# DLRM tower with a recursive field interaction: pair sums in two PSUM banks, the wide bank merged into the outer-product banks, and one of four relus moved to VectorE

## The reference, cut to what matters

```python
xk = x                                              # x: [B, 16, 256]
for i in range(3):
    z = einsum('bfe,bge->bfge', x, xk)              # all pairs of fields
    z = relu(einsum('bcl,oc->bol', z, Ws[i]) + bs[i])   # 256 pairs -> 16 outputs, for each e
    z = sum(z, axis=-1)                             # over e: [B, 16]
    outs.append(z)
    xk = broadcast(z over e)                        # [B, 16, 256]
h = concatenate([outs (48 values), dense_ctx (16)])
h = relu(h @ W_top1 + b1)                           # 64 -> 512
h = relu(h @ W_top2 + b2)                           # 512 -> 256
y = h @ W_top3                                      # 256 -> 1
```

## Time and profile before

| | |
|---|---|
| median of 3 runs | 614.34 us (613.95 to 615.65) |
| profiled execution | 614.28 us, span 612.5 us, mean granted clock 0.989 |
| PE busy | 566.3 us (92% of the span) |
| DVE busy | 494.5 us (81%) |
| ACT busy | 437.6 us (71%) |
| POOL busy | 463.1 us (76%) |

### The profile page before, as it was taken

How to read it: one execution, slowest core, us unless ns; L and a number is a source line. 1 busy time by engine, 2 the same in 40 slices (tenths; PEclk the granted TensorE clock), 3 DMA queues, 4 the chain that set the end, 5 groups by cost and what they waited for, 6 DMA issues and landing times.

```text
span 612.5 us, 18145 instructions
## 1 busy us (share of the span) xinstructions
PE 566.3 (92%) x7680; PEld 329.1 (54%) x7680; DVE 494.5 (81%) x220; ACT 437.6 (71%) x1234; POOL 463.1 (76%) x565
## 2 busy tenths in 40 slices
PE   1778889999999999999999999999999999999776
PEld 1334445555555565655556555555556565555444
DVE  5898899888888988888889888888899888887100
ACT  2466677768778776878878777887877786886542
POOL 5989888888878887888878888888878788862000
PEclk9999899999999999999999999999999999999978
DMA  4422222222222222222222122222222222210000
GB/s 98 115 76 73 62 62 71 61 62 63 61 62 63 61 63 63 61 63 61 63 63 65 58 64 62 60 63 61 63 64 63 68 61 59 59 45 1 1 1 2
DMA packets 14788, 35.89 MB, mean 59 GB/s; under 512 B 5921, under 2 KB 6305, under 8 KB 14689
## 3 DMA queue, kind: packets, MB, share of 16 engines
q0 software_dynamic: 12288, 33.57, 19.3%
q1 hardware_dynamic: 2418, 1.16, 0.8%
HBM read 34.70 MB, written 0.01 MB: 57 GB/s over the span
## 4 chain that ended last, share of the span: by engine, by line
PE 68%; DVE 20%; issue 7%; ACT 3%; POOL 2%; DMA 0%; SPq 0%; DVEq 0%; POOLq 0%; ACTq 0%
PE sum_ps L521 29%; DVE prods L222 19%; PE turn_ps L501 9%; PE outer_ps L564 9%; PE wide_ps L585 7%; PE sum_ps L541 5%; PE wide_ps L576 4%; PE outer_ps L559 3%; ACT relu_k L431 2%; POOL emb L262 2%; PE sum_ps L536 1%; PE wide_ps L593 1%; PE sum_ps L547 0%; PE sum_ps L533 0%; DMA id_lim<-id_limits 0%
## 5 line engine op out<-in xcount | busy, mean ns | idle before, releaser
L222 DVE TENSOR_TENSOR prods<-turn_ps,emb_t 128x3360 f32<-128x3360 f32 x128 | 462.2, 3646 | 11.8 <-ACT emb_t L404 8.9
L262 POOL DMA_INDIRECT emb<-tables,rows_sb x256 | 252.1, 985 | 44.9 <-issue 31.1
L521 PE MATMUL sum_ps<-prods,w_sb 128*32 128x272 f32 x4096 | 267.1, 400 | 2.5 <-POOL prods L222 2.3
L521 PEld LDWEIGHTS sum_ps<-prods,w_sb 128*32 128x32 f32 x4096 | 126.0, 110 | 94.0 <-issue 14.5
L421 ACT ACTIVATE relu<-sum_ps,bias_sb 128x120 f32<-128x120 f32 x256 | 91.8, 370 | 100.8 <-PE sum_ps L521 96.6
L272 POOL TENSOR_TENSOR prods<-emb_t 128x256 f32<-128x256 f32 x128 | 94.8, 741 | 53.8 <-ACT emb_t L404 50.3
L431 ACT ACTIVATE relu_k<-outer_ps 128x2048 f32<-128x2048 f32 x64 | 120.9, 1889 | 4.5 <-PE outer_ps L564 4.4
L501 PE MATMUL turn_ps<-ident_sb,emb 128*128 128x128 f32 x512 | 90.7, 295 | 29.7 <-DVE prods L222 10.9
L403 ACT COPY emb_t<-turn_ps 128x512 f32<-128x512 f32 x128 | 76.1, 595 | 44.2 <-PE turn_ps L501 36.2
L501 PEld LDWEIGHTS turn_ps<-ident_sb,emb 128*128 128x128 f32 x512 | 55.1, 143 | 88.8 <-issue 49.0
L411 ACT ACTIVATE prods<-emb_t 128x512 f32<-128x512 f32 x128 | 83.0, 649 | 0.1
(11 more groups left out here) (41 smaller groups left out, 269.2 us busy)
## 6 DMA issues: line engine op xcount, KB each, us to landing
emb<-tables,rows_sb POOLq DMA_INDIRECT x256
w_sb<-w_top SPq DMA_DIRECT2D x1, 512.0 KB
ids_sb<-ids_t SPq DMA_DIRECT2D x1, 128.0 KB, 2.0
h<-dense_t SPq DMA_DIRECT2D x1, 128.0 KB
w_sb<-w_top SPq DMA_DIRECT2D x1, 128.0 KB
ident_sb<-ident SPq DMA_DIRECT2D x1, 64.0 KB
w_sb<-w_cols SPq DMA_DIRECT2D x1, 64.0 KB
wp_sb<-w_proj SPq DMA_DIRECT2D x1, 32.0 KB
```

Source lines behind the costliest of these rows:

```text
L222: eng.tensor_tensor(out, every, shifted, ALU.mult).then_inc(done, 1)
L262: nc.gpsimd.indirect_dma_start(out=emb[:, k % EMB_RING, t * E:(t + 1) * E], out_offset=None, in_=tables, in_offset=bass.IndirectOffsetOnAx ...
L521: last = nc.tensor.matmul(sum_ps[s * 2 * F:(s + 1) * 2 * F, 0:SUM_COLS], w_sb[:, c, odd, :], x[:, c, 2 * s + odd, :, :], start=c == 0 and ...
```

## The change

- `wide_ps` goes. `project` writes bank 0 of `outer_ps`, the folds banks 0 and 1, `hidden1` banks 2 and 3. The waits of `wait_wide` are replaced by waits in `outer_round` and `project`.
- `sum_ps` gets two banks, by the parity of the slot; the side pieces use the bank of their slot. `turn` now waits for the sums of one slot earlier than before.
- In the second of the two layers ACT takes only the relu of the first round. A new DVE instruction, `relu_add` (slot 19, after `products`), takes the relu of the second round from the four PSUM banks and adds the first round's from SBUF (128x2048). Fold 1 then sums 8 matmuls in place of 16.
- project moves from slot 10 to 11, its transpose from 11 to 12, the second z_spread from 15 to 16, the first reduction from 15 to 16.
- `hidden1` takes its input from two copies of h0 in rows 0 to 63 and 64 to 127, and its four matmuls use the two halves of the array's rows in turn. `z_t` makes both copies with two matmuls of 64 columns, and now transposes the dense inputs too, which are loaded into `z_cat` (128 partitions x 16 groups x 16 floats) and no longer straight into h0. `w_top1` is loaded twice.
- ACT does `relu_hidden1` ahead of `take_turned` in its slot.

```diff
-PROJ, Z0_FIN, TURN_P, Z0_DIAG, Z0_SUM = 10, 9, 11, 9, 10
-Z_BUILD = (11, 15)
+PROJ, Z0_FIN, TURN_P, Z0_DIAG, Z0_SUM = 11, 9, 12, 9, 10
+Z_BUILD = (11, 16)
-REDUCE = (15, 20)
+REDUCE = (16, 20)
+RELU_ADD = 19
+PROJ_BANK, FOLD_BANK, H1_BANK = 0, (0, 1), 2
...
-        sum_ps = ps("sum_ps", [P, 512])
+        sum_ps = ps("sum_ps", [P, 2, 512])
-        wide_ps = ps("wide_ps", [P, 512])
...
-            sp.dma_start(h0[3 * F:, :], dense_t).then_inc(top_in, 16)
+            sp.dma_start(z_cat[:, :, 3 * F:], dense_b).then_inc(top_in, 16)
...
+            def relu_add(g):
+                n = ROUND_NO[1, g, 1]
+                dve.wait_ge(outer_done, n + 1)
+                dve.wait_ge(outer_relu, n)
+                at_least(dve, fold_done[1], g)
+                first, second = (relu_k[:, 1, q, :, :, :].rearrange("p j h n -> p (j h n)") for q in range(TURNS))
+                nc.vector.scalar_tensor_tensor(out=second, in0=outer_ps[:].rearrange("p j n -> p (j n)"), scalar=0.0,
+                                               in1=first, op0=ALU.max, op1=ALU.add).then_inc(outer_relu, 1)
...
-                if slot - 1 in ROUND_AT:
+                if slot - 1 in ROUND_AT and (ROUND_AT[slot - 1][0], ROUND_AT[slot - 1][2]) != (1, 1):
                     relu_round(*ROUND_AT[slot - 1])
-                take_turned(slot + 2)
                 if (g := group_at(slot - 1, HIDDEN1)) is not None:
                     relu_hidden1(g)
+                take_turned(slot + 2)
...
-                at_least(pe, relu0_ready, 3 * min(slot, STEPS))
+                at_least(pe, relu0_ready, 3 * min(slot - 1, STEPS - (slot - STEPS) % 2))
...
-                    if q == 0 and j == 1:
-                        pe.wait_ge(proj_ready, g + 1)
-                    if q == 0 and j == 2:
+                    if q == 0 and j == 0:
+                        pe.wait_ge(proj_ready if k == 0 else z_ready[0], g + 1)
+                    if q == 0 and j == 1 and k == 0:
+                        at_least(pe, z_ready[1], g)
+                    if q == 0 and j == 2 and k == 1:
+                        at_least(pe, h1_ready, H1 * g)
+                    if q == 0 and j == 3:
                         pe.wait_ge(z_wide_ready[k], g + 1)
...
-                for q in range(G4):
+                first = k * HALF_G
+                for q in range(first, G4):
...
                 for i in range(H1):
-                    last = nc.tensor.matmul(wide_ps[:, i * P:(i + 1) * P], w1_sb[:, i * P:(i + 1) * P], h0[:, g * P:(g + 1) * P],
-                                            start=True, stop=True)
+                    rows = slice(i % 2 * CAT, (i % 2 + 1) * CAT)
+                    last = nc.tensor.matmul(outer_ps[:, H1_BANK + i % 2, i // 2 * P:(i // 2 + 1) * P], w1_sb[rows, i * P:(i + 1) * P],
+                                            h0[rows, g % 2, :], start=True, stop=True)
```

More of the change, by code:

```diff
@@ L47 @@
 PT_RING = 2
-CAT_RING = 2
 LEAD = 4
@@ L190, in build @@
         N_OTHER = 3
[L192 to L198, removed]
         def wait_side(eng, slot):
-            before = [(kind, n) for at, kind, n in SIDE_ORDER if at <= slot]
-            if before:
-                kind, n = before[-1]
+            earlier = [(kind, n) for at, kind, n in SIDE_ORDER if at <= slot and (slot - at) % 2 == 0]
+            if earlier:
+                kind, n = earlier[-1]
                 done, count = {"z0": (z0_taken, n + 1), "z_t": (h0_ready, n + 1), "h2a": (h2_ready, H2 * n + 1),
@@ L380, in _ @@
                 products(slot)
+                if (g := group_at(slot, RELU_ADD)) is not None:
+                    relu_add(g)
                 if (g := group_at(slot, Z0_FIN)) is not None:
@@ L529, in side @@
                     wait_sums_read(slot)
-                    wait_side(pe, slot - 1)
+                    wait_side(pe, slot - 2)
                 if what == "z0":
                     pe.wait_ge(diag_ready, g + 1)
-                    nc.tensor.matmul(z0_ps, z0_diag[:], own_sb[:], start=True, stop=True).then_inc(z0_done, 1)
+                    nc.tensor.matmul(sum_ps[:, slot % 2, SUM_COLS:SUM_COLS + F], z0_diag[:], own_sb[:],
+                                     start=True, stop=True).then_inc(z0_done, 1)
                 elif what == "z_t":
                     pe.wait_ge(z_ready[1], g + 1)
-                    nc.tensor.matmul(z_t_ps, z_cat[:, g % CAT_RING, :], ident_sb[:], start=True, stop=True).then_inc(z_t_done, 1)
+                    for half in range(2):
+                        last = nc.tensor.matmul(sum_ps[half * CAT:(half + 1) * CAT, slot % 2, SIDE], z_cat[:, g, :], ident_sb[:],
+                                                start=True, stop=True)
+                    last.then_inc(z_t_done, 1)
                 elif what in ("h2a", "h2b"):
@@ L540, in side @@
                     for a in range(H1):
[L541 removed]
+                        last = nc.tensor.matmul(sum_ps[:, slot % 2, SIDE], w2_sb[:, a, i * P:(i + 1) * P], h1[:, a * P:(a + 1) * P],
                                                 start=a == 0, stop=a == H1 - 1)
@@ L575, in project @@
                     for j in range(J):
-                        last = nc.tensor.matmul(wide_ps[j * R:(j + 1) * R, :], wp_sb[:, c, :],
+                        last = nc.tensor.matmul(outer_ps[j * R:(j + 1) * R, PROJ_BANK, :], wp_sb[:, c, :],
                                                 x[:, j // 2, j % 2, c, :, :, 0:F], start=c == 0, stop=c == EC - 1)
@@ L621, in _ @@
                 sum_pairs(slot)
-                if slot >= STEPS and slot in WIDE_AT:
-                    wait_wide(pe, *WIDE_AT[slot])
-                by_32 = slot in WIDE_AT and WIDE_AT[slot][0] in ("proj", "fold0", "fold1")
-                if by_32:
-                    wide(*WIDE_AT[slot])
+                if (g := group_at(slot, PROJ)) is not None:
+                    project(g)
+                for k in range(2):
+                    if (g := group_at(slot, FOLD[k])) is not None:
+                        fold(k, g)
                 if slot in ROUND_AT:
                     outer_round(*ROUND_AT[slot])
-                if slot in WIDE_AT and not by_32:
-                    wide(*WIDE_AT[slot])
+                if (g := group_at(slot, HIDDEN1)) is not None:
+                    hidden1(g)
 def shape_constants():
```

87 lines of the change are left out of this document (38 added, 49 removed).

## The result

The changed kernel takes 595.59 us (median of 4 runs, 592.63 to 597.39); the kernel before took 614.82 beside it (613.95 to 615.65). The ratio is 0.968, 95% interval 0.963 to 0.973: 3.2% faster. The forecast was 589 with a range of 582 to 604, so the side and the range are right and the size is 6.6 us too hopeful. The four runs lie in two pairs, near 593 at a mean granted clock of 0.991 and near 597 at 0.983; the profiled execution is the 597.39 one, and against the control run further down its extra time is in the tail, where PE has pauses and its clock is low.

A forecast was written before the change was run, and what follows sets the result against it. PE was taken to bound the kernel, with DVE near level after the change (33.0 and 32.9 us a group). Savings of 20.7, 4.4 and 0.8 us gave a 586.6 us span, 588.4 with surroundings, rounded to 589; range 582 to 604.

The forecast's parts named there:

- relu_add, 2.20 us: On DVE, the new 2048-column instruction takes 2.20 us at the rate of products; upper bound 4.3 us.
- first rival: relu_add on DVE runs at half rate, 4.3 us: 35.3 us a group, time about 620 us; chance 0.12.
- DVE's waits give way to work: On DVE, 3.7 us a group of waits for project and the first fold are replaced by 2.2 us of work.
- Fold 1, -0.95: On PE, summing 8 matmuls in place of 16 saves half of 1.91 us, 0.95 us a group.
- The second bank of sums: No price of its own; named only as part of the possible extra gain of 0.4 us a group.
- fourth rival: More than forecast: second bank of sums and ACT's lighter load save 0.4 us a group, about 583 us; chance 0.06.
- hidden1, -0.55: On PE, hidden1's matmuls in two halves of the array nearly fully share it, saving 0.55 us a group.
- third rival: hidden1 doesn't share the array on PE: 15 x 0.55 = +8, about 597 us; chance 0.07.
- The round of the second layer: PE's round in slot 16 waits for hidden1's relus and z_wide; close to a tie, priced at 0.1 us a group.
- second rival: PE waits 0.5 to 1 us a group at the second layer's first round: about 600 us; chance 0.15.
- The period, 33.2 forecast: Groups 1 to 13 go from 34.8 to 33.2 us each, -20.7 us in all.
- Group 0, -4.4 forecast: Group 0 keeps DVE's busy 30.25 us plus some 1 us for ACT's copies: -4.4 us from 35.6.
- After the groups, -0.8 forecast: Six slots after 538.3 us gain from the sooner reduction but lose relu_add: -0.8 us; the tail's -0.6 taken as 0.

The follow-up runs named there:

- control run: The changed kernel unaltered, run again on the same chip as the runs beside it: 595.25 us, ratio 0.971 to the kernel before.
- act_relu: The changed kernel with the fourth round's relu back on ACT and fold 1 summing all 16 matmuls: 600.39 us, ratio 0.982 to the kernel before.
- both_fixes: The changed kernel with finish0's single reduction and the tail's outputs in turn_ps together: 583.17 us, ratio 0.963 to the kernel before.
- add_twice: The changed kernel with relu_add done twice, the first result into a spare buffer: 633.90 us, ratio 1.036 to the kernel before.
- relu_add_alone: The kernel before with only relu_add on DVE at slot 19 and fold 1 halved to 8 matmuls: 621.72 us, ratio 1.015.
- reduce_15: The changed kernel with the first reduction and second z_spread back in slot 15: 610.81 us, ratio 0.995 to the kernel before.
- one_sum_bank: The changed kernel with sum_ps back in one bank and its waits as before: 609.16 us, ratio 1.004 to the kernel before.
- copies_first: The changed kernel with ACT doing take_turned ahead of relu_hidden1 again: 593.72 us, ratio 0.979 to the kernel before.
- one_reduce: The changed kernel with finish0's two DVE instructions replaced by one reduction over 17 columns: 591.03 us, ratio 0.963 to the kernel before.
- tail_banks: The changed kernel with hidden1 of the last three groups and the last project writing turn_ps: 589.31 us, ratio 0.961 to the kernel before.
- port_probe: The changed kernel with one more 16-column DVE product, SBUF to SBUF, after each products, 128 in all: 607.93 us in one execution.

## Why the prediction was right, and where its sum was off

*What bounds the kernel.* PE before, PE and DVE level after: as said. `act_relu` shows PE busy 33.85 of 33.85 and `both_fixes` 32.90 of 32.90, and the forecast of PE's own work was 33.0 us (33.11 busy in the period above). DVE's forecast of 32.9 met its busy time of 32.99 partly by luck: 0.4 of that is the hold of `z_rows`, which I didn't know, and the rest is 0.3 less than I had summed.

*relu_add, 2.20 us.* Measured 2.20 from start to start, 2.28 as its own duration. The first rival is settled: with one source in PSUM and one in SBUF it goes at the 1.04 ns a column of `products`. The Trainium skill, "Vector Engine (DVE) Microarchitecture Reference", section 7, halves this form for two non-bf16 SBUF sources. With one in PSUM the runs show no halving. `add_twice` shows what it would have cost: 3.6% slower.

*DVE's waits give way to work.* Right, no wait for project or the first fold is left. But the prediction told the moves as one item. `relu_add_alone` and `reduce_15` show that the reduction's slot is what makes room: without it the kernel takes 1.5% more and 0.5% less than before.

*Fold 1, -0.95.* Right: 2.00 us to the next start before (305.57 to 307.57), 1.10 after and 1.00 in `both_fixes`.

*The merged bank adds nothing.* Right in the groups. It is also what allows the reduction's move: with one `wide_ps`, hidden1 in slot 15 would have to wait for a reduction in slot 16. That is read from the order of the uses, not tried.

*The second bank of sums.* The prediction names it only in the fourth rival, as a possible extra. The forecast silently took "the side pieces stay as they are" for granted; `one_sum_bank` shows that without this bank they don't, for 0.85 us a group. It takes 15.4 us more than `copies_first`, which ran beside it; 595.6 + 15.4 is 611 us, an estimate, and outside my range. The forecast came out right because the change had the bank, not because I had worked that term out: luck. The fourth rival's extra gain didn't come.

*hidden1, -0.55.* Measured -0.45 (1.09 to 0.64), so the third rival fell. The estimate of -0.41 from the Trainium skill's figure ("TensorE: Matmul & The Clock Gate", part 3) was the closer. It cost 0.1 us a group. My reading of the rounds as nearly fully shared was too high: durations of records overlap without sharing too. hidden1's own eight of 289 ns, 2.3 us, stood in 1.18 us in the earlier trace rows, so the rounds' 6.0 us in 1.03 are a sharing of about 3 of 4, an estimate from these two rows.

*The round of the second layer.* I put 0.1 us a group on the tie; from 100 us on the trace has 0.3 us in one group. The second rival fell in the groups. In the tail, where there are no steps to cover them, the same waits stand.

*The period, 33.2 forecast, 33.45 measured: the largest miss, 4.8 of 20.7 us over the thirteen groups.* A part of it is group 1, which takes 34.52 us (82.73 to 117.25) and has PE's wait of 2.2 us for z_wide in it; the twelve others take 33.49. There DVE's row has 32.6 us of its own work, 0.41 of waiting for ACT's copies and 0.4 by which `z_rows` is held by POOL. The copies I knew from the earlier trace rows and let them be covered. The hold I did not know. `one_reduce` takes the held instruction away and gets 33.18, the forecast's figure, though with less work on DVE than the forecast had. The prediction's "hand-overs that I didn't see" had 0.6 us in the whole sum and needed over 4.

*Group 0, -4.4 forecast, -2.5 measured.* I had left DVE its work and 1 us of waiting. It had 30.83 us of work, 0.8 of it in a `z_rows` of 0.97 us that POOL held, and waited 2.3 us for project. PE came late to project, with waits for POOL before it. From 20 to 95 us:

```profile
PE sum_ps L520 <- POOL prods L208: 7.6, 9, 1.0
...
DVE proj_b L355 <- PE outer_ps L587: 2.3, 1, 2.3
PE outer_ps L568 <- POOL z_wide L283: 2.2, 1, 2.2
```

Of the first row 1.8 us are in this group and 5.8 in the 30 us ahead of it; the last row is in group 1. POOL is busy 30.26 us of this group's 33.14. That POOL is what holds group 0 up rests on the profile alone; no run tests it.

*After the groups, -0.8 forecast, +2.3 in the profiled execution.* The tail's rows:

```profile
549.80 0.39 PE L568 MATMUL outer_ps<-bias_wide,ones_sb 32*128 32x512 bf16 x2 [1.28 <-ACT h L457]
...
554.37 2.29 DVE L365 SCALAR_TENSOR_TENSOR relu_k<-outer_ps,relu_k 128x2048 f32<-128x2048 f32 x1 [5.10 <-PE outer_ps L573]
556.71 3.14 PE L587 MATMUL outer_ps<-emb_t,wp_sb 128*32 128x512 f32 x16 [2.10 <-DVE relu_k L365]
559.60 1.59 PE L597 MATMUL outer_ps<-relu_k,fold_sb 128*32 128x256 f32 x16
...
575.62 0.39 PE L568 MATMUL outer_ps<-bias_wide,ones_sb 32*128 32x512 bf16 x2 [0.92 <-ACT h L457]
```

project stood 2.10 us behind relu_add, for which I had 1.4; the relus of hidden1 cost 1.28 and 0.92, for which I had 1.5; and project itself then took 2.89 us at a granted clock of 0.60, where `tail_banks`, without the wait, has 1.93 at 1.00. That is a term that I didn't have. The two halved folds (fold 1) gave back 1.8 us, for which I had 2.7: 1.87 and 3.33 us before, 1.52 and 1.86 after, again at a low clock (0.64 and 0.50). So the forecast listed the waits and made the two largest too small. `tail_banks`, which removes them, shows that they cost 4.7 us in the profile with what the low clock adds (5.9 by the medians). The execution-to-execution difference of the changed kernel is here too: 48.1 us at a granted clock of 0.81 in this profile, 45.4 at 0.89 in the control's. Why the clock falls more often in one execution than in another stays open.

The sum: of the 9.0 us between the forecast span change (-25.9) and the profiled one (-16.9), the groups are 4.8, group 0 is 1.9 and what follows them 3.1, less 0.8 that the start gained.

## What to carry to other kernels

When two engines are nearly level, add up the idle time of the one that gets the new work and ask for each wait in it which edit removes it: here the work for DVE cost 1.5% by itself, and the whole change was worth 0.5% without the move of one reduction by a slot, 3% with it. When a piece is moved, look also at what it used to cover in its old slot, since that cover may be the only reason for which a shared buffer was cheap. And when waits in the body are hidden by a stream of steps, price them a second time for the tail, where they stand bare.

## What the runs showed of the hardware

- A DVE instruction with both sources in SBUF, started in the middle of a POOL tensor_tensor, ends 0.03 to 0.05 us after POOL's (`port_probe`). Started with 0.14 us or less of it left it wasn't held by it, but one probe that did so (62.36 us) was caught by POOL's next instruction, which started 0.08 us later, and took 1.18 us. Bare it takes 0.15 to 0.18. In the changed kernel `z_rows` reached 0.97 us that way, at the end of group 0, started 0.12 us into a `z_wide` of 1.04. `products` and relu_add, with one source in PSUM, showed no such stretch: where the changed kernel's timeline shows them singly, from 60 to 540 us, they took 3.63 to 3.66 and 2.27 to 2.28 us. The Trainium skill, "SBUF — State Buffer", section "SBUF: two separate sides", describes this as a pair of ports that the two engines hold exclusively, for a whole instruction, and says that a DVE instruction with two SBUF inputs takes part only against POOL instructions that read SBUF. The probes agree for tensor_tensor.
- For POOL's indirect gather the picture is mixed: probes that started in its first 0.31 us took 0.14 to 0.19 us, those 0.42 and 0.55 us into it 0.56 and 0.57, and those in its last 0.2 us 0.16 to 0.24; a `z_rows` of the kernel before, 0.37 us into one, took 0.62. The `z_rows` at 317.96 is of the second kind: it started 0.56 us into a gather (317.40, 0.98 long) and took 0.55. So a shift of 0.4 us in where the two meet cost this kernel 0.4 us a group. No run here separates what part of the gather holds the instruction up.
- Four matmuls of 64 rows by 128 columns, in turn in the two halves of the rows: 0.64 us against 1.09 one behind the other, a factor of 1.7.
